# Keys and values in two sets of buffers and half a group ahead, in an eight-group decoder kernel on one core

## The chip, the cores and the metric

The kernel runs on one core of a Trainium2 chip. Its engines are TensorE (PE), VectorE (DVE), ScalarE (ACT), GpSimd (POOL) and SyncE (SP, which issues the DMAs); each takes its own instructions in order and waits on semaphores. The metric is the device time of one execution in microseconds. PE's granted clock is 2.4 GHz (1.00 in the rows) or 1.2 GHz (0.50).

## The reference

Two post-norm decoder layers over x of 16 x 128 x 256, with a context `ctx_2048` of the same shape. Each line is one of six stages:

```python
x = _layernorm(x + _L0_attn_ref(x, qkv, o_proj, gamma, beta))        # causal attention, one head of 256
x = _layernorm(x + _L0_xattn_ref(x, k, fside_S2_0, ctx, ctx, 8))     # long convolution, 8 x 8 products
x = _layernorm(x + _L0_ffn_ref(x, w1, g1, w2, g2, w3, g3))           # int8 activations, ternary weights
x = _layernorm(x + _L1_attn_ref(x, Wr, Wk, Wv, Wo, decay, ...))      # decayed running sum of k * v
x = _layernorm(x + _L1_xattn_ref(x, ctx, mask, Wq, bq, Wk, bk, ...)) # 16 query heads, 4 key/value heads of 128
x = _layernorm(x + _L1_ffn_ref(x, w_gating, w_linear))               # fp8 gated FFN
```

The cross attention of layer 1 is what the change touches most. Its keys and values come from the context alone; only the queries need x:

```python
q = (hidden_states @ Wq + bq)...; k = (encoder_hidden_states @ Wk + bk)...; v = (encoder_hidden_states @ Wv + bv)...
q = _rmsnorm(q, qn_w); k = _rmsnorm(k, kn_w)
probs = softmax(q @ k.T * scale + attention_mask); out = (probs @ v) @ Wo
```

The ternary weights of the layer-0 FFN are `round(tanh(w / mean|w|))`, that is -1, 0 or 1, times one scale.

## The kernel before

The 16 sequences go in 8 groups of 2 (GB = 2); a group has 256 rows. There are three stations, and each holds another group at the same time. Station a does a group's layer-0 attention and convolution (`front`), and later its last FFN (`ffn`, three groups behind: AHEAD = 4). Station c (`middle`) does the ternary FFN (steps c_) and the running sum (steps d_). Station e does the cross attention: `keys_queries` (letter q: keys, values, queries), `scores` for each sequence of the group (letters x and y) and `output` (letter o).

For every engine, each station is a generator that yields between steps, and `together` plays the generators in the order of a string of letters, `ORDER[engine]`. The strings are written out in the file (one letter a step) and set what stands behind what on each in-order engine. The eight PSUM banks are split: A0, A1 (banks 0, 1) for station a, C0, C1 (2, 3) for c, E0, E1 (4, 5) for the scores, EQ (6) for keys, values and queries, EY (7) for the output product.

Station q, one group before the change: two key products into EQ (L1159), DVE adds the bias into KX (L884), POOL squares KX into QS (L411), DVE sums (L887), POOL takes the power and scales KX (L414, L416); then the group's rows are turned (L966), the first quarter of the queries is made (L1166) with its sums of squares (L1171, L1177), the scaled keys are turned (L1224) and copied to KTX by ScalarE (L586), and the two value products follow (L1159, copied to VX in L595); then the other three quarters of queries. KX, KTX, VX and QS exist once. QS is also where ScalarE puts the squares of the queries. All steps of q go through the one bank EQ, each waiting for the last one to be read out.

Station c for a group: DVE scales and quantises the rows (L766 to L780), PE turns them (L1098), four pairs of matmuls make gate and value of a hidden quarter in C0 and C1 (L1111), each pair waiting for DVE to have read the last (c_h); ScalarE takes tanh (L536), DVE forms the hidden values (L788, L789); POOL multiplies by g3 (L394), DVE quantises (L794 to L806), PE turns and multiplies by w_dn (L1118, L1124), DVE adds and norms. Then the running sum: projections (L972, L1138), K1 from ScalarE, times the value projection on DVE (L828), times dinv on POOL (L402), running sum on PE (L1144), means (L1148, L1151), output projection and the second norm.

At the start the weights are loaded and prepared through two stage buffers that share memory with station e's tiles: the ternary weights as bf16 (L449, L454, L641) and the weights of the last FFN as fp8 (L469). `keep_clock` puts small matmuls on PE where it would be quiet; the last 56 of them stand right behind the last output product.

## Time and profile before

| | us |
|---|---|
| median of 3 runs | 922.15 |
| lowest and highest | 920.11, 922.54 |
| the profiled execution | 919.01 |
| its span, first to last instruction | 917.2 |
| PE busy | 832.2 (91%) |
| DVE, ACT, POOL busy | 685.5 (75%), 518.5 (57%), 297.4 (32%) |
| mean granted PE clock | 0.976 |

Start times in the rows count from the start of the span. A row of the order in time has start, duration, engine, line, operation, tiles written and read, and in square brackets the idle time before it with the releaser. Four fp32 matmuls show as eight records.

### The profile page before, as it was taken

How to read it: one execution, taken by the hardware profiler on the slowest of the kernel's cores; microseconds unless marked ns; L12 is line 12 of the kernel's file. 1: busy time of each engine (PE TensorE's matmuls, PEld its weight loads, DVE VectorE, ACT ScalarE, POOL GpSimd, SP SyncE). 2: the span in 40 equal slices, each digit the busy share in tenths (PEclk: the TensorE clock that was granted, in tenths of full speed). 3: DMA queues.
4: the chain of work that ended last, by engine and by line, in shares of the span. 5: the costliest groups of instructions: out<-in, count | busy, mean ns of one | idle time of the engine just before them, and what ended most of it. 6: DMA issues, size and time to landing. Idle time of an engine off the chain costs nothing.

```text
span 917.2 us, 14519 instructions
## 1 busy us (share of the span) xinstructions
PE 832.2 (91%) x5052; PEld 646.5 (70%) x5068; DVE 685.5 (75%) x1687; ACT 518.5 (57%) x1317; POOL 297.4 (32%) x314
## 2 busy tenths in 40 slices
PE   6866958999899999999999999999999998999984
PEld 5743845886687667876689677786689766686763
DVE  2777767978896887786968869687968979483544
ACT  4464127525436775358752695527863487576853
POOL 0426314522622252514233423351235423230110
PEclk9986979999999999999999999999999999999998
DMA  8780100010010000010001000000000000000000
GB/s 279 252 285 31 24 1 24 1 24 1 12 30 7 12 1 24 1 24 2 24 12 24 1 1 24 12 12 14 24 1 1 1 12 13 1 1 13 1 12 12
DMA packets 37063, 28.66 MB, mean 31 GB/s; under 512 B 18688, under 2 KB 34560, under 8 KB 36608
## 3 DMA queue, kind: packets, MB, share of 16 engines
q1 hardware_dynamic: 36992, 27.74, 9.8%
q8 instruction: 41, 0.67, 0.3%
q14 instruction: 30, 0.25, 0.1%
HBM read 25.64 MB, written 2.10 MB: 30 GB/s over the span
## 4 chain that ended last, share of the span: by engine, by line
PE 56%; DVE 27%; ACT 7%; issue 6%; POOL 2%; DMA 1%; DVEq 0%; SPq 0%; POOLq 0%; ACTq 0%
PE bank L1166 7%; PE bank L1262 6%; PE bank L972 5%; PE bank L1159 4%; PE bank L1251 4%; PE bank L1241 3%; DVE S L900 3%; PE bank L1073 2%; PE bank L1043 2%; PE bank L1041 2%; PE bank L1044 2%; PE bank L1246 2%; PE bank L1111 2%; PE bank L1171 2%; DVE S L907 2%
## 5 line engine op out<-in xcount | busy, mean ns | idle before, releaser
L606 ACT ACTIVATE S<-S,mx 128x128 f32<-128x128 f32 x256 | 99.5, 394 | 46.1 <-DVE mx L903 45.9
L1166 PE MATMUL bank<-XTE,w_xq 128*128 128x256 f32 x512 | 122.6, 382 | 1.4 <-ACT QA L565 0.7
L1262 PE MATMUL bank<-w_xo,OX 128*128 128x256 f32 x512 | 116.1, 380 | 0.9 <-ACT OX L615 0.9
L1166 PEld LDWEIGHTS bank<-XTE,w_xq 128*128 128x128 f32 x512 | 93.9, 190 | 17.5 <-ACT QA L565 3.1
L1262 PEld LDWEIGHTS bank<-w_xo,OX 128*128 128x128 f32 x512 | 95.0, 190 | 13.9 <-issue 2.1
L564 ACT ACTIVATE QS<-bank,per_partition_sb 128x256 f32<-128x256 f32 x128 | 60.6, 473 | 62.4 <-PE bank L1166 62.3
L338 POOL TENSOR_TENSOR rq<-vq,minus_half 128x8 f32<-128x8 f32 x32 | 53.7, 1679 | 123.3 <-DVE vq L879 123.2
L900 DVE SCALAR_TENSOR_TENSOR S<-bank,rq,xmask 128x128 f32<-128x128 f32 x256 | 71.7, 342 | 19.8 <-PE bank L1241 17.8
L236 POOL TENSOR_TENSOR prod<-XTA,ccolA 128x256 f32<-128x256 f32 x96 | 60.7, 664 | 45.0 <-PE bank L1044 25.0
L1241 PEld LDWEIGHTS bank<-KTX,QA 128*128 128x128 f32 x512 | 63.3, 192 | 12.3 <-issue 10.7
L1241 PE MATMUL bank<-KTX,QA 128*128 128x128 f32 x512 | 67.8, 278 | 1.0 <-ACT OX L615 0.9
L615 ACT ACTIVATE OX<-bank,bv_sb 128x512 f32<-128x512 f32 x64 | 44.0, 691 | 42.2 <-PE bank L1251 30.2
L1159 PE MATMUL bank<-w_xkv_sb,ccolE 128*128 128x512 f32 x128 | 62.2, 609 | 4.6 <-DMA w_xo<-in_L_xattn_Wo 3.4
L1251 PE MATMUL bank<-PT,VX 128*128 128x512 f32 x128 | 65.6, 603 | 0.3 <-ACT PT L610 0.3
L565 ACT ACTIVATE QA<-bank,per_partition_sb 128x256 f32<-128x256 f32 x128 | 60.8, 475 | 0.0
L394 POOL TENSOR_TENSOR H<-H,g 128x1024 f32<-128x1024 f32 x16 | 38.5, 2403 | 58.3 <-ACT Q L540 58.3
L338 POOL TENSOR_TENSOR rstd_c<-veps_c,minus_half 128x2 f32<-128x2 f32 x24 | 16.9, 705 | 111.0 <-DVE veps_c L667 98.2
L907 DVE TENSOR_TENSOR S<-S,rs 128x512 f32<-128x512 f32 x64 | 51.2, 801 | 2.2
L1043 PE MATMUL bank<-prod,taps_sb 128*128 128x128 f32 x256 | 51.2, 282 | 1.3 <-DVE Zc L720 1.3
L1044 PE MATMUL bank<-prod,taps_sb 128*128 128x128 f32 x256 | 50.4, 279 | 0.0
L606 ACT ACTIVATION_READ_ACCUMULATOR S<-S,mx 128x1 f32 x256 | 49.1, 192 | 0.0
L610 ACT ACTIVATE PT<-bank 128x512 f32<-128x512 f32 x64 | 37.8, 601 | 19.9 <-PE bank L1246 19.8
(225 smaller groups left out, 1852.5 us busy)
## 6 DMA issues: line engine op xcount, KB each, us to landing
xin<-in_x SPq DMA_DIRECT2D x8, 256.0 KB, 2.7
taps_sb<-in_taps SPq DMA_DIRECT2D x1, 2048.0 KB, 11.8
cnat<-in_ctx SPq DMA_DIRECT2D x8, 256.0 KB, 2.7
ccolA<-in_ctxT SPq DMA_DIRECT2D x32, 64.0 KB, 2.7
ccolE<-in_ctxT SPq DMA_DIRECT2D x16, 128.0 KB, 2.3
w_xq<-in_L_xattn_Wq SPq DMA_DIRECT2D x1, 2048.0 KB, 13.1
w_xo<-in_L_xattn_Wo SPq DMA_DIRECT2D x1, 2048.0 KB, 17.8
out_x<-X SPq DMA_DIRECT2D x8, 256.0 KB, 2.1
```

Of the source, the lines that this page charges most:

```text
L338: sig(gp.tensor_tensor(out, src, minus_half[:, 0:n], ALU.pow), name)
L565: ins = nc.scalar.activation(QA[:, n % 2, h], q, ACT.Identity, bias=bq[:, hh:hh + 1])
L606: ins = nc.scalar.activation(S[:, b, seq(h)], S[:, b, seq(h)], ACT.Exp, bias=mx[:, b, h:h + 1], accum_out=sm[:, b, h:h + 1])
L900: ins = nc.vector.scalar_tensor_tensor(s3[:, h], EB[b][:, seq(h)], rq[:, n % 2, b * XGROUP + h:b * XGROUP + h + 1], xmask[:], ALU.mult, AL ...
L907: sig(nc.vector.tensor_tensor(s3, s3, rs[:, b].unsqueeze(2).broadcast_to([P, XGROUP, P]), ALU.mult), f"e_p{b}")
L1043: nc.tensor.matmul(out[:, :, h], taps[:, hq * 4 + h, 0:P], mv_[:, 1], start=True, stop=False)
L1044: ins = nc.tensor.matmul(out[:, :, h], taps[:, hq * 4 + h, P:], mv_[:, 0], start=False, stop=True)
L1159: ins = nc.tensor.matmul(EQ[:], ccolE[:, k, b], w_xkv[:, k, v], start=k == 0, stop=k == HALVES - 1)
L1166: ins = nc.tensor.matmul(cols(EQ)[:, h], w_xq[:, k, hh * XDIM:(hh + 1) * XDIM], XTE[:, k], start=k == 0, stop=k == HALVES - 1)
L1241: ins = nc.tensor.matmul(EB[b][:, seq(h)], QA[:, n % 2, h, seq(b)], KTX[:, b, n], start=True, stop=True)
L1251: sig(nc.tensor.matmul(EB[b][:], VX[:, b, n * XDIM:(n + 1) * XDIM], PT[:, b], start=True, stop=True), f"e_o{b}")
L1262: ins = nc.tensor.matmul(rows(EY)[:, b], OX[:, h, b], w_xo[:, n * XGROUP + h], start=n == 0 and h == 0 and b == 0, stop=n == XKV - 1 and h ...
```

## The change

- KTX and VX exist twice, one set for even and one for odd groups (`KTX[g % 2]`, `VX[g % 2]`). The set for odd groups shares memory with the weight stages as before.
- `keys_queries` is split into `keys(g, half)` and `queries(g, n)`. `station_q` plays keys and values of groups 0 and 1 first, before any query; then, in each group g from 1 to 6, group g + 1's key products behind query quarter 1 and its key transposes and value products behind quarter 2. The waits are moved to match: the key sums e_vk of the next group are waited for by ScalarE before quarter 2.
- `w_gv` and `w_dn` are fp8 instead of bf16, with saturate=False where they are written.
- In group 0 the hidden quarters 1 and 3 go to E0 and EY instead of C0 and C1, so a quarter waits for the one two before it.
- K1 is multiplied by dinv on POOL first and by the value projection on DVE after it.
- All five order strings are new.

```diff
-        w_gv, w_dn = sb("w_gv", [2, HALVES, HIDDEN], BF), sb("w_dn", [FFN_K, DIM], BF)
+        w_gv, w_dn = sb("w_gv", [2, HALVES, HIDDEN], F8), sb("w_dn", [FFN_K, DIM], F8)
...
+        KTX, VX = (sb("KTX0", [GB, XKV, P]), t["KTX1"]), (sb("VX0", [GB, BANK]), t["VX1"])
...
+        def hidden_banks(g, j):
+
+            return (E0, EY) if g == 0 and j % 2 else (C0, C1)
+
+        def hidden_free(g, j):
+
+            return j - 2 if g == 0 else j - 1
...
+        def keys_made_with(g):
+
+            return g + 1 if 1 <= g < GROUPS - 1 else None
+
+        def station_q(keys, queries):
+            for g in range(2):
+                yield from keys(g, 0)
+                yield from keys(g, 1)
+            for g in range(GROUPS):
+                made = keys_made_with(g)
+                for n in range(XKV):
+                    yield from queries(g, n)
+                    if made and n in (1, 2):
+                        yield from keys(made, n - 1)
...
-                gp.wait_ge(sems["d_kv"], nth(g))
-                sig(gp.tensor_tensor(K1[:], K1[:], dinv[:].unsqueeze(1).broadcast_to([P, GB, DIM]), ALU.mult), "d_kvs")
+                gp.wait_ge(sems["d_k"], nth(g))
+                sig(gp.tensor_tensor(K1[:], K1[:], dinv[:].unsqueeze(1).broadcast_to([P, GB, DIM]), ALU.mult), "d_kd")
...
+                    if n == 0 and pr == 0 and g == 0:
+                        act.wait_ge(sems["e_vk"], nth(1))
+                    if n == 2 and pr == 0 and made:
+                        act.wait_ge(sems["e_vk"], nth(made))
...
-                    else:
-                        pe.wait_ge(sems["c_h"], nth(g, 2 * GB, j - 1))
+                    if hidden_free(g, j) >= 0:
+                        pe.wait_ge(sems["c_h"], nth(g, 2 * GB, hidden_free(g, j)))
...
+                    if g == 0:
+                        pe.wait_ge(sems["e_kTc"], nth(1, GB, 1))
+                    else:
+                        pe.wait_ge(sems["e_vq"], nth(g - 1, XKV, XKV - 1))
+                    transpose_rows(X[g % XBUF], EQ, "e_xT")
```

How the order strings move instructions, at three places. PE at the start, behind the last instruction of set-up (the turned decay, L960 before and L995 now). L1111 and L1146 are group 0's hidden quarters, L1159 and L1194 key and value products, L991, L972 and L999 (L1026, L1007, L1034) group 1's attention. Before:

```order
58 L960 MATMUL bank5<-ident,dscale 128x128 x2
59 L1159 MATMUL bank6<-w_xkv_sb,ccolE 128x512 x2
60 L1098 MATMUL bank2<-ident_bf,QQ 128x128 x8
61 L966 MATMUL bank0<-ident,Z 128x128 x4
62 L1159 MATMUL bank6<-w_xkv_sb,ccolE 128x512 x2
63 L1111 MATMUL bank2<-w_gv,QQ 128x512 x2
64 L1111 MATMUL bank3<-w_gv,QQ 128x512 x2
65 L991 MATMUL bank1<-XTA,w_qk 128x256 x4
66 L972 MATMUL bank0<-w_vo,XTA 128x256 x4
67 L999 MATMUL bank1<-XTA,QT 128x128 x4
68 L1111 MATMUL bank2<-w_gv,QQ 128x512 x2
69 L1111 MATMUL bank3<-w_gv,QQ 128x512 x2
```

and now:

```order
59 L1133 MATMUL bank2<-ident_bf,QQ 128x128 x8
60 L1194 MATMUL bank6<-w_xkv_sb,ccolE 128x512 x2
61 L1146 MATMUL bank2<-w_gv,QQ 128x512 x2
62 L1146 MATMUL bank3<-w_gv,QQ 128x512 x2
63 L1146 MATMUL bank4<-w_gv,QQ 128x512 x2
64 L1146 MATMUL bank7<-w_gv,QQ 128x512 x2
65 L1001 MATMUL bank0<-ident,Z 128x128 x4
66 L1194 MATMUL bank6<-w_xkv_sb,ccolE 128x512 x2
67 L1146 MATMUL bank2<-w_gv,QQ 128x512 x2
68 L1146 MATMUL bank3<-w_gv,QQ 128x512 x2
69 L1146 MATMUL bank4<-w_gv,QQ 128x512 x2
70 L1146 MATMUL bank7<-w_gv,QQ 128x512 x2
```

Two hidden quarters now stand next to each other, in four banks, ahead of group 1's attention. Further on, the value products and key transposes of group 0 and the key and value products of group 1 (L1194, L1224) stand between group 0's remaining steps.

POOL at the start, from group 1's convolution products (prod, L236 before and L260 now) to the second norm of group 0. Before:

```order
43 L236 TENSOR_TENSOR prod<-XTA,ccolA 128x256 x3
44 L378 TENSOR_TENSOR UA<-X1,SK 128x512
45 L338 TENSOR_TENSOR rstd_c<-veps_c,minus_half 128x2
46 L402 TENSOR_TENSOR K1<-K1,dinv 128x512
47 L338 TENSOR_TENSOR rstd_a<-veps_a,minus_half 128x2 x2
48 L338 TENSOR_TENSOR rstd_c<-veps_c,minus_half 128x2
49 L338 TENSOR_TENSOR rstd_c<-veps_c,minus_half 128x2
```

and now:

```order
40 L362 TENSOR_TENSOR rstd_c<-veps_c,minus_half 128x2
41 L437 TENSOR_TENSOR QS<-KX 128x1024
42 L260 TENSOR_TENSOR prod<-XTA,ccolA 128x256
43 L260 TENSOR_TENSOR prod<-XTA,ccolA 128x256 x3
44 L260 TENSOR_TENSOR prod<-XTA,ccolA 128x256
45 L260 TENSOR_TENSOR prod<-XTA,ccolA 128x256 x3
46 L426 TENSOR_TENSOR K1<-K1,dinv 128x512
47 L402 TENSOR_TENSOR UA<-X1,SK 128x512
48 L440 TENSOR_TENSOR rk<-vk,minus_half 128x8
49 L442 TENSOR_TENSOR KX<-KX,rk 128x1024
50 L362 TENSOR_TENSOR rstd_c<-veps_c,minus_half 128x2
51 L362 TENSOR_TENSOR rstd_c<-veps_c,minus_half 128x2
```

Group 1's key steps (L437, L440, L442) have come in, and group 0's first norm stands ahead of two thirds of group 1's convolution products instead of behind them.

PE at the end. L1262 and L1317 are output products (bank 7), L978 and L1013 the clock keepers, L1080 and L1115 the transposes and L1087 and L1122 the products of the last FFN. Before:

```order
1038 L1251 MATMUL bank5<-PT,VX 128x512
1039 L1262 MATMUL bank7<-w_xo,OX 128x256 x8
1040 L978 MATMUL bank6<-ident_bf 128x128 x56
1041 L966 MATMUL bank0<-ident,X2 128x128 x4
1042 L1073 MATMUL bank0<-w_gf,X8 128x512 x2
```

and now:

```order
1031 L1306 MATMUL bank5<-PT,VX1 128x512
1032 L1108 MATMUL bank0<-w_gf,X8 128x512 x2
1033 L1108 MATMUL bank1<-w_gf,X8 128x512 x2
1034 L1317 MATMUL bank7<-w_xo,OX 128x256 x8
1035 L1013 MATMUL bank6<-ident_bf 128x128 x56
1036 L1115 MATMUL bank0<-ident_bf,G16 128x128 x8
1037 L1115 MATMUL bank1<-ident_bf,G16 128x128 x8
1038 L1122 MATMUL bank0<-w_ln,A8T 128x256 x8
1039 L1122 MATMUL bank1<-w_ln,A8T 128x256 x8
1040 L1001 MATMUL bank0<-ident,X2 128x128 x4
```

The second half of group 6's last FFN now stands behind the last output product, ahead of group 7's FFN, whose first transpose (into bank 0, from X2) waits for group 6's norm.

## Rows read from the trace of the kernel before

**Rows 1.** Page, part 1: busy time and share of the span.

```profile
PE 832.2 (91%) x5052; PEld 646.5 (70%) x5068; DVE 685.5 (75%) x1687; ACT 518.5 (57%) x1317; POOL 297.4 (32%) x314
```

**Rows 2.** Stretches: length, busy time by engine (records), PE clock, DMA share, GB/s.

```profile
0.00:138.00 138.00, 97.99 (x621) 79.83 (x623) 90.53 (x217) 51.13 (x88) 45.01 (x62) 0.86 0.44 145
138.00:893.00 755.00, 721.89 (x4325) 558.43 (x4339) 584.65 (x1445) 459.02 (x1218) 251.01 (x250) 1.00 0.04 11
893.00:917.20 24.20, 12.37 (x110) 8.25 (x108) 10.35 (x25) 8.39 (x12) 1.39 (x2) 0.86 0.03 12
...
54.50:132.00 77.50, 55.70 (x274) 42.16 (x276) 54.97 (x132) 22.48 (x40) 29.88 (x34) 0.78 0.19 57
...
127.59:132.61 5.02, 5.02 (x26) 4.41 (x24) 3.60 (x10) 1.71 (x6) 0.70 (x2) 0.87 0.00 0
```

**Rows 3.** Order in time, group 0 through station c, to its queries.

```profile
54.49 1.29 DVE L766 TENSOR_TENSOR UG<-X,g 128x512 f32<-128x512 f32 x2
...
60.62 0.69 DVE L780 TENSOR_SCALAR QQ<-UG 128x1024 bf16<-128x1024 f32 x1
...
84.70 1.88 DVE L803 TENSOR_TENSOR fac<-fac,srms 128x1 f32<-128x1 f32 x1
...
87.47 0.69 DVE L806 TENSOR_SCALAR Q<-H 128x1024 bf16<-128x1024 f32 x1
...
105.38 0.73 DVE L672 TENSOR_SCALAR X<-UC,mv_c,rstd_c 128x256 f32<-128x256 f32 x2
...
130.73 0.74 DVE L672 TENSOR_SCALAR X<-UC,mv_c,rstd_c 128x256 f32<-128x256 f32 x2 [0.81 <-POOL rstd_c L338]
...
133.90 1.99 PE L1166 MATMUL bank<-XTE,w_xq 128*128 128x256 f32 x8 [0.69 <-ACT XTE L570]
```

**Rows 4.** PE's waits from 138 to 893 us: total, times, longest.

```profile
PE bank L1224 <- ACT KTX L586: 2.0, 3, 0.9
```

**Rows 5.** PE by group: count, busy us, mean ns, idle before; last, the chain.

```profile
L1159 PE MATMUL bank<-w_xkv_sb,ccolE 128*128 128x512 f32 x128 | 62.2, 609 | 4.6 <-DMA w_xo<-in_L_xattn_Wo 3.4 <-DVE vq L879 0.6 <-ACT KTX L586 0.3
...
L1073 PE MATMUL bank<-w_gf,X 128*128 128x512 fp8e4 x128 | 32.3, 379 | 2.1 <-ACT X L500 1.5 <-DVE F L742 0.5
L1111 PE MATMUL bank<-w_gv,QQ 128*128 128x512 bf16 x112 | 30.2, 387 | 7.5 <-DVE H L789 3.9 <-ACT QQ L531 2.9
...
L1224 PE MATMUL bank<-ident,KX 128*128 128x128 f32 x64 | 9.8, 275 | 2.0 <-ACT KTX L586 2.0
...
351.94 1.72 PE bank L1159 x4
```

**Rows 6.** POOL and DVE: steps of the keys, and the two that meet at 84 us.

```profile
L416 POOL TENSOR_TENSOR KX<-KX,rk 128x1024 f32<-128x1024 f32 x8 | 15.2, 1897 | 0.6
L411 POOL TENSOR_TENSOR QS<-KX 128x1024 f32<-128x1024 f32 x8 | 15.2, 1894 | 36.8 <-DVE KX L884 36.8
L414 POOL TENSOR_TENSOR rk<-vk,minus_half 128x8 f32<-128x8 f32 x8 | 13.7, 1711 | 10.1 <-DVE vk L888 10.1
...
L887 DVE TENSOR_REDUCE vk<-QS 128x8 f32<-128x1024 f32 x8 | 9.7, 1213 | 5.2 <-POOL QS L411 5.2
...
84.23 2.34 POOL L394 TENSOR_TENSOR H<-H,g 128x1024 f32<-128x1024 f32 x1
...
L803 DVE TENSOR_TENSOR fac<-fac,srms x16: 158/159/1953, 84.7 to 769.4; 128x1 f32<-128x1 f32 x16
```

**Rows 7.** Order in time at the end.

```profile
876.81 1.04 PE L1087 MATMUL bank<-w_ln,A8T 128*128 128x256 fp8e4 x8
...
893.20 3.29 PE L978 MATMUL bank<-ident_bf 128*128 128x128 bf16 x56
...
897.17 0.63 PE L966 MATMUL bank<-ident,X 128*128 128x128 f32 x4 [0.68 <-DVE X L672]
...
907.12 3.56 PE L1087 MATMUL bank<-w_ln,A8T 128*128 128x256 fp8e4 x16
...
913.79 0.73 DVE L672 TENSOR_SCALAR X<-UA,mv_g,rstd_g 128x256 f32<-128x256 f32 x2 [0.81 <-POOL rstd_g L338]
```

More of the change, by code:

```diff
@@ L406, in middle, with keys @@
                 yield from norm(g, "c", 1, 2)
-            def keys_queries(g):
+            def keys(g, half):
+                if half == 1:
+                    return
                 yield
@@ L616, in scores @@
                                              bias=bv[:, n:n + 1]), f"e_oc{b}")
-            together(ORDER["act"], s=set_up(), a=station_a(front, ffn), c=each_group(middle), q=each_group(keys_queries),
+            together(ORDER["act"], s=set_up(), a=station_a(front, ffn), c=each_group(middle), q=station_q(keys, queries),
                      x=each_group(lambda g: scores(g, 0)), y=each_group(lambda g: scores(g, 1)))
@@ L888, in keys_queries, with queries @@
                 sig(nc.vector.tensor_scalar(vk[:], vk[:], 1.0 / XDIM, 1e-6, ALU.mult, ALU.add), "e_vk")
-                yield from query_squares(0)
-                for n in range(1, XKV):
-                    yield from query_squares(n)
+            def queries(g, n):
+                yield
+                dve.wait_ge(sems["e_ssT"], nth(g, XKV, n))
+                if g or n >= 2:
+                    dve.wait_ge(sems["e_rq"], g * XKV + n - 1)
+                sums = EQ[:, 0:GB * P].rearrange("p (m r) -> p m r", r=QUARTER)[:, :, 0]
+                sig(nc.vector.tensor_scalar(vq[:, n % 2], sums, 1.0 / XDIM, 1e-6, ALU.mult, ALU.add), "e_vq")
             def scores(g, b):
@@ L918, in output @@
                 norm_out("e", UE, x)
-            together(ORDER["dve"], s=set_up(), a=station_a(front, ffn), c=each_group(middle), q=each_group(keys_queries),
+            together(ORDER["dve"], s=set_up(), a=station_a(front, ffn), c=each_group(middle), q=station_q(keys, queries),
                      x=each_group(lambda g: scores(g, 0)), y=each_group(lambda g: scores(g, 1)), o=each_group(output))
@@ L1154, in middle, with keys, product @@
                 project_rows(C1, lambda k, b: NT[:, b, k], lambda k: w_o1[:, k], "d_y")
-            def keys_queries(g):
-                def keys_values(v, b):
+            def keys(g, half):
+                def product(v, b):
                     for k in range(HALVES):
@@ new lines, in keys_turned @@
+                def keys_turned():
+                    for b in range(GB):
+                        yield
+                        if b == 1:
+                            pe.wait_ge(sems["e_kTc"], nth(g, GB, 0))
+                        elif g < 2:
+                            pe.wait_ge(sems["e_vc"], nth(g, GB, 1))
+                        else:
+                            pe.wait_ge(sems["e_vq"], nth(g - 1, XKV, 2))
+                        if b == 0:
+                            pe.wait_ge(sems["e_kn"], nth(g))
+                        for m in range(XKV):
+                            ins = nc.tensor.transpose(EQ[:, seq(m)], KX[:, b, m * XDIM:(m + 1) * XDIM], ident[:])
+                        sig(ins, "e_kT")
@@ new lines, in values @@
+                def values():
+                    for b in range(GB):
+                        yield
+                        if b == 1:
+                            pe.wait_ge(sems["e_vc"], nth(g, GB, 0))
+                        elif g < 2:
+                            pe.wait_ge(sems["e_kc"], nth(g, GB, 1))
+                        else:
+                            pe.wait_ge(sems["e_kTc"], nth(g, GB, 1))
+                        product(1, b)
+                if half == 0:
+                    yield from keys_made()
+                    if g < 2:
+                        yield from values()
+                else:
+                    yield from keys_turned()
+                    if g >= 2:
+                        yield from values()
@@ new lines, in queries @@
+                yield
+                pe.wait_ge(sems["e_qc"], nth(g, 2 * XKV, 2 * n + 1))
+                for h in range(XGROUP):
+                    ins = nc.tensor.matmul(EQ[h * QUARTER:(h + 1) * QUARTER, 0:GB * P], ones[:, 0:QUARTER], QS[:, h], start=True, stop=True)
+                sig(ins, "e_ssq")
+                yield
+                pe.wait_ge(sems["e_ssc"], nth(g, XKV, n))
+                for b in range(GB):
+                    ins = nc.tensor.transpose(EQ[:, seq(b)], SSQ[:, seq(b)], ident[:])
@@ L1240, in scores @@
                     for h in range(XGROUP):
[L1241 removed]
+                        ins = nc.tensor.matmul(EB[b][:, seq(h)], QA[:, n % 2, h, seq(b)], KTX[g % 2][:, b, n], start=True, stop=True)
                     sig(ins, f"e_sc{b}")
@@ L1268, in output @@
                         keep_clock(EQ, 56)
-            together(ORDER["pe"], s=set_up(), a=station_a(front, ffn), c=each_group(middle), q=each_group(keys_queries),
+            together(ORDER["pe"], s=set_up(), a=station_a(front, ffn), c=each_group(middle), q=station_q(keys, queries),
                      x=each_group(lambda g: scores(g, 0)), y=each_group(lambda g: scores(g, 1)), o=each_group(output))
```

267 lines of the change are left out of this document (120 added, 147 removed).

## The prediction, before the result was known

> **What bounds the kernel now.** I read the page first: TensorE (PE) is busy for 832.2 us, 91% of the span, VectorE (DVE) for 75% [rows 1]. The table of stretches says where the missing 9% lies. From 0 to 138 us PE is busy for 97.99, so idle for 40.0, at a mean granted clock of 0.86. From 138 to 893 us it is busy for 721.89 of 755, idle for 33.1 (4.4%), at full clock. In the last 24.2 us it is idle for 11.8 [rows 2]. The middle is a PE stage; start and end are chains. So an edit pays if it takes waiting out of the start or end, or if it puts PE work of the middle into waiting at the start; shortening a chain in the middle is worth at most its part of 33.1 us.
>
> The order in time shows the chain of the start, which runs through DVE. Station c takes group 0's rows at 54.49; its first quantised hidden half is there at 88.16 (start 87.47 plus 0.69); its first norm is written from 105.38 and its second from 130.73, right behind which group 1's station c starts; PE starts group 0's queries at 133.90 [rows 3]. From 54.5 to 132 us PE is busy for 55.70 of 77.5, at a clock of 0.78 [rows 2]. In the middle, from 138 to 893 us, the list of waits shows little before key and value steps: 2.0 us in all before the key transposes [rows 4].
>
> **The change, part by part.** My sum goes against the profiled execution, 919.0 us (span 917.2 and 1.8 around it). The median of the three runs is 922.15, 3.1 above; I put the difference onto the median.
>
> *Two groups' keys and values in front.* A group's eight products take 62.2 / 8 = 7.8 us of PE, its transposes 9.8 / 8 = 1.2 [rows 5]. Up to the start of group 0's queries PE now does, beyond what it did before, group 0's value products and key transposes and all of group 1's: (3.9 + 1.2) + (7.8 + 1.2) = 14.1 us by busy time. These sums count overlapping ends: a product of four records is 1.94 by this count and 1.72 on the chain [rows 5], so I take 14.1 x 1.72 / 1.94 = 12.5. Group 2's first projections and scores, 5.0 us on PE [rows 2], have moved behind. Net, 7.5 us of work leave the PE-bound part.
>
> *Group 0's hidden layer in four banks, and the order around it.* Before, each of four matmul groups waited for VectorE to finish the one before, with group 1's attention between. Now the first two run back to back, and quantising the first half comes ahead of group 1's residual. I walked the new order by hand with durations from the trace. Quantised input 60.4 (before 61.3 [rows 3]; a norm of group 1 no longer stands in it). First products end near 66, hidden quarters written at 67.0, 68.5, 73.5 and 74.9. Two things hold it up: ScalarE now has the weight copies behind the first activation, so the stage loads start about 5 us later, and POOL has group 0's key work (1.89 + 1.71 + 1.90 [rows 6]) between its two g3 products of 2.4. Still the quantised halves come at 79.5 and 86.3, the first before at 88.2, and the first norm at about 96 instead of 105.4. From there the new order is slower than the old: station d's steps share DVE with twelve convolution steps of group 1, which before were finished. On the other side K1 is multiplied by dinv (a POOL step) while PE makes the second projection, and not behind it, which saves about 1.2 on the chain. I get the second norm at 119 to 120 instead of 130.7, queries at 120.3 instead of 133.9, and group 1's station c at 121.5. Allowing for a half clock (1.2 instead of 2.4 GHz) on PE where it starts from quiet, for which the 0.78 of before stands, I take 11.5 us, bounds 6 and 14.
>
> *Less to fill with.* The work moved forward was filler behind 138 us. With 7.5 us of it gone and the chains earlier by unequal amounts (queries 13.6 us, group 1's station c 10, group 2's front hardly), some idleness returns. It can't be below 0 by this reason, nor much above the 7.5 and the spread of 4 to 5 between the chains, 12. I take 5, that spread.
>
> *Keys half a group ahead.* Number and kind of steps through bank EQ are the same, so PE's and DVE's sums stay. Scores of a group can start once its first queries are out. Gain at most 2 us or so, the waits of [rows 4]; the loss is a rival below. I take 0.
>
> *Ternary weights as fp8.* They are the moving operand. L1073 with fp8 and L1111 with bf16, both 512 columns, take 32.3 / 128 = 0.25 and 30.2 / 112 = 0.27 us busy [rows 5], so the two differ by 0.02 x 128 = 2.6 us over the kernel, part of which is the slower clock under the first ones. No row has mixed operands; a loss of that size is in the range.
>
> *The end.* Before, group 6's FFN was through when the last output product ended at 893.36; behind it came 56 clock keepers, then group 7's FFN at 897.17 [rows 7]. Now group 6's two transposes and two products stand between the keepers and group 7's FFN. The chain: last output product end + 3.2 (keepers) + 1.1 (transposes) + 0.7 and 1.02 (ScalarE, second half ends) + 1.04 (product) + 3.8 from the last product to the written norm (910.68 to 914.52 before [rows 7]) + 0.1 = 11.0 us, against 3.8 before: +7.1. The 3.1 us of PE work (1.06 and twice 1.04) leave the part ahead. Net +4.0 if PE bounds there, +7.1 if it doesn't. I take 4.
>
> **The sum:** -11.5 - 7.5 + 5 + 0 + 0 + 4.0 = -10.0 us. That is 909.0 for a profiled execution and 912.1, say **912 us**, for the median.
>
> **A rule weighed.** In the trace one DVE step of one element per partition (fac, L803; median 159 ns, longest 1953) lasts 1.88 us at 84.70: it ends at 86.58, just when POOL's product over H (84.23 plus 2.34) ends [rows 3, 6]. The change puts 5.5 us more of POOL work into the start, so up to two such holds (3.8 us) can be added on the chain. By this the sum would be -6.2, 916. The Trainium skill says in GPSIMD Engine Reference, section Specifications, that POOL's SBUF interface is shared with VectorE, with contention for instructions that have two SBUF inputs. The trace agrees for this row. I keep it as a rival, because the row has a median of 159.
>
> **The rivals.**
> - *The fill holds.* Group 0's queries and scores come together with group 1's hidden layer and group 2's front, so no idleness returns (-5), and the waits before key steps go (-2): 922.15 - 17.0 = 905. For it: three independent stations are open from 121 us on. Against: all three lean on DVE, 75% busy [rows 1].
> - *The fill is lost.* Idleness of 12 instead of 5 comes back: 922.15 - 3.0 = 919, at the edge of what is measurable.
> - *Keys in the middle of a group stall the queries (slower).* ScalarE may not write the squares of query quarter 2 before the next group's key sums are out, and the transposes wait for scaled keys: 1.89 + 1.38 + 1.71 + 1.90 = 6.9 us of POOL and DVE work [rows 6], the 1.38 being DVE's reduction of 1.21 and a small step, in groups 1 to 6, with the remaining scores of the group queued behind on PE. Before, this wait lay at the group's start, where the last group's scores covered it. At 3 us uncovered in each of six groups: +18, 930. It decides from 10.0 / 6 = 1.7 us a group. Against: PE has waited for little in the middle.
> - *The keys don't get out of the way.* Group 0's rows can't be turned into queries before group 1's keys are through bank EQ; POOL scales them behind two convolution products and dinv. By my walk they are through at 116, 3 us ahead. If they end 4 us late, 916.
> - *POOL holds VectorE*, above: 916.
>
> **How the numbers follow.** Forecast 0.41, fill holds 0.22, fill lost 0.15, slower by stalled queries 0.12, keys in the way 0.06, POOL holds 0.04. A measurement tells 0.3%, 2.8 us, from no change. Faster: 0.41 + 0.22 + 0.06 + 0.04 = 0.73; same 0.15; slower 0.12. The range goes from 903 (fill holds, 2 us of the startup's upper bound) to 925 (fill lost, the fp8 loss and the end at +7.1); it leaves out the slower case and little else.
>
> **What would show it.** In the changed profile: group 0's queries start near 120 us and the stretch before it has PE idle of about 20 and not 40 us; PE's idle time in the middle near 38; group 7's FFN starts 11 us behind the end of the last output product. If queries start at 130 or later, the walk is wrong. If they start at 120 and the time doesn't fall, the fill is. If PE waits for QS or KX in every group, the slower rival holds.

## The result: 900.4 us, and the profile of the changed kernel

The changed kernel takes 900.38 us (median), the kernel before 921.89 in the same comparison: a ratio of 0.977, interval 0.9745 to 0.9786. It is faster, as forecast, but by 21.5 us and not by 10, and so below the low end of the range (903). One of its four executions took 4810.06 us and counts in the median but not in the ratio; the other three, 899.28 to 900.97, have a median of 899.80, so differences below that are taken from 900.38 would be 0.6 us more from there. The profiled execution has a span of 897.5 us against 917.2, 19.7 less.

First the page of the changed kernel, part 1 (busy time, share of the span, instructions), which answers [rows 1]:

```profile
PE 825.7 (92%) x5068; PEld 642.1 (72%) x5068; DVE 692.7 (77%) x1687; ACT 515.9 (57%) x1315; POOL 296.2 (33%) x314
```

TensorE still bounds the kernel. Where the time went is read from stretches cut at the same events in both kernels: 54.5 us (station c takes group 0's rows), the start of group 0's queries, the end of the last output product, the end. Up to 54.5 us both are alike. The columns are those of [rows 2]. First before:

```profile
54.50:133.90 79.40, 56.91 (x284) 43.14 (x285) 56.83 (x134) 23.96 (x43) 30.92 (x36) 0.79 0.18 56
133.90:893.36 759.46, 725.05 (x4344) 560.89 (x4360) 588.43 (x1459) 460.75 (x1222) 251.01 (x250) 1.00 0.04 11
893.36:917.20 23.84, 12.01 (x109) 8.00 (x105) 10.35 (x25) 8.39 (x12) 1.39 (x2) 0.86 0.03 12
```

Then the changed kernel:

```profile
54.50:128.06 73.56, 54.11 (x297) 38.27 (x297) 59.84 (x137) 26.28 (x47) 33.80 (x38) 0.94 0.23 67
128.06:866.76 738.70, 717.12 (x4315) 559.00 (x4316) 589.12 (x1447) 454.52 (x1215) 245.69 (x248) 0.99 0.04 10
866.76:897.50 30.74, 16.32 (x141) 10.21 (x137) 14.50 (x38) 9.63 (x14) 2.47 (x3) 0.84 0.05 18
```

The start is 5.8 us shorter, the middle 20.8 us, the end 6.9 us longer. In the middle, TensorE is busy 7.9 us less (725.05 to 717.12) and idle 12.8 us less: 759.46 - 725.05 = 34.4 before, 738.70 - 717.12 = 21.6 now. The prediction had idle time rising by 5 there. That is the miss to explain. (The trace before lacks 16 records of L1111, 5052 against 5068 weight loads [rows 1]; by the gaps at their places they would fill between 1 and 2 us of the 34.4, so it is not made by them.) TensorE's busy time there fell by less than forecast, 7.9 us and not 10.6 (7.5 moved to the front, 3.1 to the end).

The order in time of the start on VectorE, which answers [rows 3]:

```profile
60.41 0.69 DVE L815 TENSOR_SCALAR QQ<-UG 128x1024 bf16<-128x1024 f32 x1
...
72.68 1.22 DVE L917 TENSOR_REDUCE vk<-QS 128x8 f32<-128x1024 f32 x1 [2.01 <-POOL QS L437]
73.93 1.05 DVE L918 TENSOR_SCALAR vk<-vk 128x8 f32<-128x8 f32 x1
...
79.69 2.10 DVE L836 TENSOR_TENSOR deq<-amax,srms 128x1 f32<-128x1 f32 x1
...
83.26 0.69 DVE L842 TENSOR_SCALAR Q<-H 128x1024 bf16<-128x1024 f32 x1
...
89.11 0.69 DVE L842 TENSOR_SCALAR Q<-H 128x1024 bf16<-128x1024 f32 x1
...
98.73 2.23 DVE L707 TENSOR_SCALAR X<-UC,mv_c,rstd_c 128x256 f32<-128x256 f32 x2
...
124.79 0.73 DVE L707 TENSOR_SCALAR X<-UC,mv_c,rstd_c 128x256 f32<-128x256 f32 x2
```

The chain has the links that the prediction walked, each later than walked: the quantised input is through at 61.1 (walked: 60.4), the quantised halves at 84.0 and 89.8 (79.5 and 86.3); the first norm starts at 98.7 (96), the second at 124.8 (119 to 120), the queries at 128.06 (120.3). From the start of the quantised input to the queries it takes 67.65 us, against 73.28 before (60.62 to 133.90 [rows 3]).

TensorE's order in time goes on:

```profile
128.06 3.78 PE L1275 MATMUL bank<-XTE,w_xq 128*128 128x256 f32 x8 [1.82 <-ACT XTE L618]
...
133.50 3.72 PE L1275 MATMUL bank<-XTE,w_xq 128*128 128x256 f32 x8 [0.81 <-ACT QA L630]
```

Eight such records took 1.99 us before [rows 3]. The granted clock is 0.50 from 128.06 to 136.00, where before it is 1.00 from 133.90 on: the new order has little on TensorE right ahead of the queries (0.66 us of work from 124 to 128.06), the old one had group 1's attention there. These 7.94 us hold 7.1 us of busy time, of which the half clock costs about 3.6 (an estimate: the same products took about half in the kernel before). That is more than the 2.7 us by which the fall in busy time fell short.

### The profile page after: what moved, and what is told of

It is laid out like the page before. It is cut to its first block, busy times and chain, and to the rows that moved or that the text cites. A ratio compares the mean times of both kernels' runs of the same rounds, so it can differ in the third digit from the quotient of the medians.

```text
span 897.5 us, 14530 instructions
## 1 busy us (share of the span) xinstructions
PE 825.7 (92%) x5068; PEld 642.1 (72%) x5068; DVE 692.7 (77%) x1687; ACT 515.9 (57%) x1315; POOL 296.2 (33%) x314
## 4 chain that ended last, share of the span: by engine, by line
PE 61%; DVE 21%; ACT 9%; issue 5%; DMA 1%; POOL 1%; SPq 0%; POOLq 0%; DVEq 0%; ACTq 0%
PE bank L1317 9%; PE bank L1275 8%; PE bank L1007 5%; PE bank L1194 4%; PE bank L1306 4%; PE bank L1296 4%; PE bank L1078 2%; PE bank L1301 2%; PE bank L1079 2%; PE bank L1076 2%; PE bank L1108 2%; DVE amax L830 2%; DVE S L935 1%; PE bank L1280 1%; ACT S L641 1%
## 5 line engine op out<-in xcount | busy, mean ns | idle before, releaser
L1275 PE MATMUL bank<-XTE,w_xq 128*128 128x256 f32 x512 | 126.2, 390 | 5.4 <-ACT QA L630 2.7
L1317 PE MATMUL bank<-w_xo,OX 128*128 128x256 f32 x512 | 116.0, 380 | 0.0
L1275 PEld LDWEIGHTS bank<-XTE,w_xq 128*128 128x128 f32 x512 | 96.2, 194 | 22.8 <-ACT QA L630 5.6
L1317 PEld LDWEIGHTS bank<-w_xo,OX 128*128 128x128 f32 x512 | 95.4, 190 | 14.0 <-issue 1.8
L260 POOL TENSOR_TENSOR prod<-XTA,ccolA 128x256 f32<-128x256 f32 x96 | 60.4, 661 | 26.6 <-DVE prod L260 16.8
L1194 PE MATMUL bank<-w_xkv_sb,ccolE 128*128 128x512 f32 x128 | 62.7, 613 | 1.1 <-ACT KTX L591 0.9
L1078 PE MATMUL bank<-prod,taps_sb 128*128 128x128 f32 x256 | 50.0, 277 | 1.5 <-DVE SK L747 1.0
L1079 PE MATMUL bank<-prod,taps_sb 128*128 128x128 f32 x256 | 49.5, 275 | 0.0
L755 DVE TENSOR_TENSOR Zc<-bank,ccolA 128x512 f32<-128x512 f32 x64 | 43.7, 683 | 7.3 <-PE bank L1079 4.4
```

The source lines that it names most:

```text
L1078: nc.tensor.matmul(out[:, :, h], taps[:, hq * 4 + h, 0:P], mv_[:, 1], start=True, stop=False)
L1079: ins = nc.tensor.matmul(out[:, :, h], taps[:, hq * 4 + h, P:], mv_[:, 0], start=False, stop=True)
L1194: ins = nc.tensor.matmul(EQ[:], ccolE[:, k, b], w_xkv[:, k, v], start=k == 0, stop=k == HALVES - 1)
L1275: ins = nc.tensor.matmul(cols(EQ)[:, h], w_xq[:, k, hh * XDIM:(hh + 1) * XDIM], XTE[:, k], start=k == 0, stop=k == HALVES - 1)
L1317: ins = nc.tensor.matmul(rows(EY)[:, b], OX[:, h, b], w_xo[:, n * XGROUP + h], start=n == 0 and h == 0 and b == 0, stop=n == XKV - 1 and h ...
```

## The experiments

Order strings are quoted only where a few letters say what moved. The start of the same instructions varies by several microseconds between executions (last section), so a loss there is read from the quantised input on. "Middle" is always from the start of group 0's queries to the end of the last output product.

**The two borrowed banks.** Group 0's hidden layer goes back to two banks, all order strings as they are.

```diff
-            return (E0, EY) if g == 0 and j % 2 else (C0, C1)
+            return (C0, C1)
-            return j - 2 if g == 0 else j - 1
+            return j - 1
```

> The changed kernel with group 0's hidden layer back in two banks (C0, C1) instead of four, same order. Each of its four matmul groups waits for VectorE to have read the one before. If the borrowed banks carry the earlier start (5.8 us measured), the start of group 0's queries comes 4 to 6 us later and the whole 2 to 5 us later, 902 to 905. If VectorE sets the pace there anyhow (a hidden quarter takes it 1.4 us and TensorE under a microsecond), under 1.5 us is lost: 900 to 902.

Measured: 909.98 us, ratio to the kernel before 0.988 (0.9855 to 0.9904), so 9.6 us over the changed kernel. The order in time of its VectorE shows where:

```profile
62.12 0.69 DVE L815 TENSOR_SCALAR QQ<-UG 128x1024 bf16<-128x1024 f32 x1
...
80.53 0.68 DVE L824 SCALAR_TENSOR_TENSOR SW<-SW,bank 128x512 f32<-128x512 f32 x1
...
95.45 0.69 DVE L842 TENSOR_SCALAR Q<-H 128x1024 bf16<-128x1024 f32 x1
```

From quantised input to first quantised half it takes 33.3 us, against 22.9 with four banks. Queries start at 140.15, and the middle is 738.85 us long against 738.70: the whole loss, 12.1 us between the two profiles, lies in the start and is carried to the end undiminished. The quantised input itself comes 1.7 us later, which the edit doesn't touch; the link to the first half accounts for the other 10.5. Both readings in the expectation were too low. I had counted what VectorE needs for a quarter, 1.4 us. TensorE's order in time in the same kernel shows a round trip instead:

```profile
70.73 1.78 PE L1146 MATMUL bank<-w_gv,QQ 128*128 128x512 fp8e4 x4 [2.38 <-DVE H L825]
...
75.43 1.03 PE L1146 MATMUL bank<-w_gv,QQ 128*128 128x512 fp8e4 x4
82.14 1.86 PE L1146 MATMUL bank<-w_gv,QQ 128*128 128x512 fp8e4 x4 [5.69 <-DVE H L825]
```

The second and the fourth quarter wait for VectorE (2.38 and 5.69 us), and behind the wait their products run at half clock (1.78 and 1.86 us for four, at a granted clock of 0.53 and 0.50, against 1.03 us at 1.00). The second wait is long since VectorE had the sums of the key squares ahead of the third quarter. The order strings stand as they were made for four banks, with two quarters next to each other, so this is what the banks are worth in this order; an order made for two banks wasn't tried.

**Group 1's keys not in front.** Only group 0's keys and values are made in front; group 1's are made among group 0's queries. Where a step didn't have to move, it kept its place.

```diff
-            return g + 1 if 1 <= g < GROUPS - 1 else None
+            return g + 1 if g < GROUPS - 1 else None
...
-            for g in range(2):
-                yield from keys(g, 0)
-                yield from keys(g, 1)
+            yield from keys(0, 0)
+            yield from keys(0, 1)
```

> The changed kernel with only group 0's keys and values in front; group 1's stand among group 0's queries, as those of the later groups do. The order of all other steps is that of the changed kernel. The prediction's term for the work moved to the front: group 1's share is 9.0 of 14.1 us, so about 8 us of TensorE work go back behind the start. If that work filled idle time in front (the prediction's view), the time is 5 to 8 us longer, 905 to 908, with queries of group 0 starting earlier or at the same 128. If the idle time in the middle takes the work in again (there are 21.6 us of it), under 3 us: 900 to 903.

Measured: 913.57 us, ratio 0.992 (0.9902 to 0.994), 13.2 us over the changed kernel. Its middle and end:

```profile
127.60:881.35 753.75, 726.01 (x4336) 562.78 (x4337) 592.22 (x1451) 456.34 (x1219) 251.96 (x251) 0.99 0.04 10
881.35:912.20 30.85, 16.47 (x141) 10.50 (x139) 14.67 (x38) 9.79 (x14) 2.47 (x3) 0.84 0.05 18
```

Queries start at 127.6, and 66.7 us behind the quantised input where the changed kernel takes 67.65: group 1's keys in front cost the start about 1 us. The middle is 15.1 us longer: 8.9 us are work (726.01 against 717.12), and 6.2 us are *more* idle time (27.7 against 21.6). The list of TensorE's waits in its middle names them (total, times, longest):

```profile
PE bank L1193 <- DVE KX L913: 3.6, 1, 3.6
...
PE bank L1272 <- DVE KX L913: 0.9, 1, 0.9
PE bank L1193 <- ACT KTX L593: 0.8, 1, 0.8
PE bank L1193 <- ACT VX L601: 0.7, 1, 0.7
PE bank L1272 <- ACT VX L601: 0.7, 1, 0.7
```

These five, 6.7 us together, are waits of or behind key and value steps (L1193 is the product for keys and values, L1272 the query projection behind it). The list of the changed kernel's middle, which goes down to 0.4 us, has none of them. So group 1's keys and values, made here, bring waits beside their work, and in front they cost next to none. The prediction's bound, that idle time can't fall when this work goes, fails on this.

How much of it lies in the steps and how much in their place is not shown. The same steps of groups 2 to 7 stand in the changed kernel's middle without a listed wait, and in the kernel before, key and value steps account for 3.2 us of TensorE's waits in the whole middle (2.0 before the key transposes [rows 4], 1.2 before L1159). Group 1's stand at 161 to 206 us, among group 0's queries, in strings that are otherwise made for a kernel without them there. Another place for them was not tried, so a less fitting order remains a rival for the 6.2 us.

One more reading. Middle and end together are 753.75 + 30.85 = 784.6 us here, and 759.46 + 23.84 = 783.3 in the kernel before. With group 1's keys out of the front, the rest of the change (two sets of buffers, later groups' keys half a group ahead, new orders) gains nothing behind the start in this order: the middle is 5.7 us shorter than before (753.75 against 759.46), and the end 7.0 us longer.

**Where the later groups' keys stand.** Three pairs of kernels. In each, both have an order made by the same procedure from durations of the trace; one has the program of the changed kernel, the other makes keys and values of group g (from 2 on) between the last queries of group g-1 and the first of its own. Both sets of buffers stay.

```diff
                 for n in range(XKV):
                     yield from queries(g, n)
-                    if made and n in (1, 2):
-                        yield from keys(made, n - 1)
+                if made:
+                    yield from keys(made, 0)
+                    yield from keys(made, 1)
```

> The changed kernel (keys half a group ahead, two sets of buffers, four banks for group 0) with all five order strings made anew by a search of my own; computation and steps are the same, only their interleaving differs. It is the partner of n_start, whose order was made by the same search. If the change's own order strings were the source of the 12.8 us of TensorE idle time that left the middle, another order has no reason to keep it: 905 to 920. If the structure gives the slack, an order from an unrelated search keeps it: 885 to 900, with idle time in the middle at or below the 21.6 us of the changed kernel.

> As n_after, with an order from the same search, but the keys and values of group g (g from 2) are made between the last queries of group g-1 and the first of group g, not among the queries of g-1. Buffers stay double. Theory A (keys in the middle of a group fill waits, and free the start of each group from a chain of 6.9 us of POOL and DVE steps): 8 to 12 us longer than n_after, with waits of TensorE before key transposes or at the first queries of a group. Theory B (where the keys stand doesn't matter, only that the order is good): within 3 us of n_after.

> As n_after, with the order of a second, independent search (another seed). It measures how much of the time hangs on the search's luck: if order luck is a few us, 908 to 920.

> As n_start (keys and values of a group between the last queries of the group ahead and the first of its own), with the order of a second, independent search. Theory A (keys among the queries give 10 us or more by structure): slower than both n_after and n_after2, 920 to 935. Theory B (the 14.5 us between n_after and n_start were the luck of one order): it lies among them, 908 to 920.

> The changed kernel with an order that keeps its own as the priority, but lets a step go ahead where, on durations from the trace, the one in front of it isn't ready. Partner of g_start. If the changed kernel's order is near the best for its structure, this is 0 to 10 us slower, 900 to 910.

> Same rule and same priorities as g_after, with the keys and values of a group (from 2 on) between the last queries of the group ahead and its own first ones. Theory A (keys half a group ahead give slack by structure): 7 to 15 us slower than g_after, as in the two pairs before. Theory B: within 4 us of it.

Measured, in us; the ratio is to the kernel before.

| pair | keys among the queries | keys at the group's start | difference of medians | of middle and end, by the traces |
|---|---|---|---|---|
| n | 914.46 (0.993; 0.9909 to 0.9948) | 928.91 (1.010; 1.0063 to 1.0131) | 14.4 | 19.7 |
| n, second order | 919.72 (1.000; 0.9985 to 1.0007) | 927.20 (1.007; 1.0059 to 1.0089) | 7.5 | 2.0 |
| g | 928.81 (1.009; 1.0062 to 1.0126) | 965.16 (1.049; 1.0447 to 1.0526) | 36.3 | 37.1 |

The last column leaves the start out: in the second pair 7.1 of the difference is a later start (queries at 140.7 and not 133.6). The middle of the third pair:

```profile
131.80:895.40 763.60, 723.55 (x4312) 559.58 (x4313) 587.20 (x1445) 453.17 (x1215) 244.42 (x247) 0.99 0.04 10
```

```profile
131.60:938.60 807.00, 743.05 (x4344) 566.31 (x4345) 592.59 (x1464) 459.15 (x1222) 245.93 (x250) 0.97 0.04 10
```

The first fence is the one with keys among the queries, the second the one with keys at the start of the group: 64 us of idle time in the middle against 40. In the list of waits of the second, TensorE waits 9.1 us before key and value steps for ScalarE's copy of the turned keys (6.0 at L1193, 3.1 at L1223); that of the first has no such row.

Two things follow. All three differences have one sign, so keys half a group ahead are no burden and may be a help; but 2.0, 19.7 and 37.1 are no size, and this stays open. And one program with four orders (the changed kernel's and three of mine) has 769.4, 780.3, 783.0 and 794.4 us in middle and end: the order strings alone are worth 11 to 25 us. My expectation that an unrelated order would keep the small idle time (at or below 21.6 us, and 885 to 900 in all) held for none: the first n kernel comes nearest in the middle with 24.3 us, g has 40.1. The 914.46 of the first lies in the range that was given for order strings as the source, 905 to 920.

**The dinv product.** POOL's product of K1 and dinv stands behind VectorE's product of keys and values again.

```diff
-                gp.wait_ge(sems["d_k"], nth(g))
+                gp.wait_ge(sems["d_kv"], nth(g))
...
-                dve.wait_ge(sems["d_kd"], nth(g))
+                dve.wait_ge(sems["d_k"], nth(g))
...
-                pe.wait_ge(sems["d_kv"], nth(g))
+                pe.wait_ge(sems["d_kd"], nth(g))
```

> The changed kernel with POOL's product of K1 and dinv (1.26 us) behind VectorE's product of keys and values again, as in the kernel before; order strings as in the changed kernel. The prediction gave the swap 1.2 us on group 0's chain and nothing elsewhere: +1 to +1.5 us, 901 to 902. If in each group this chain is where waits of TensorE come from, 1.2 us in each of eight groups would show: up to +6, 906.

Measured: 904.74 us, ratio 0.984 (0.9806 to 0.9868), 4.4 us over the changed kernel, between the two expectations. TensorE's wait ahead of the state product, as that line's own view gives it, in this kernel and in the changed one (the first row is the line's operations, the second what its engine waited for, us and times):

```profile
L1179 PE MATMUL bank<-upto,K x64: 275/275/377, 111.7 to 773.6; 128*128 128x128 f32 x64
...
  POOL K L426: 6.3, 4
```

```profile
L1179 PE MATMUL bank<-upto,K x64: 273/275/377, 109.6 to 767.6; 128*128 128x128 f32 x64
...
  DVE K L864: 1.5, 2
```

The swap takes 4.8 us of waits at this line away over eight groups. The middle is 3.4 us shorter with it (738.70 against 742.10), and from quantised input to queries it takes 67.65 us against 68.65, 1.0 less. The prediction gave it 1.2 us in the start, which is borne out, and looked no further.

**The start's key steps.** This one was meant to let group 0's hidden quarters and g3 products go ahead of its key squares.

The first letters of POOL's string; those of TensorE, VectorE and ScalarE have changes of this size too.

```diff
-sasaaaaaaacsaqcqcaaacqaacaqccacaqaac
+sasaaaaaaacasqcqcaaacaqcaaqccacaqaac
```

> As e_tail (keepers behind group 6's FFN, its second FFN half ahead of the residual sum), and in the start four short pieces of the order strings changed, one on each of TensorE, VectorE, ScalarE and POOL: group 0's key squares and sums (POOL 1.89 and 1.66 + 1.90 us, VectorE 1.21 + 1.05) give way to group 0's hidden quarters and its g3 products. In the changed kernel they stood between them: POOL started the g3 product at 72.6 although the quarters were there at 70.1, VectorE waited 2.0 us for POOL's squares with a hidden quarter queued behind, and deq lasted 2.10 us. If this is the part of the start that the prediction missed (5.8 us gained instead of 11.5), group 0's queries start 4 to 7 us earlier than e_tail's 127.2, and the time is 890 to 893 against 896.3. If the start is bound by something else (the 20 us of station d behind the first norm), the queries stay at 126 to 128 and the time at 895 to 897.

Measured: 899.25 us, ratio 0.977 (0.9754 to 0.9783), which is 3 us *more* than e_tail (below, from which it is made), queries at 130.1 instead of 127.2. But the edit didn't do what the expectation says: in the strings that ran, letters moved around the squares and not past them, and the trace has them where they were (VectorE waits 2.01 us for POOL's squares at 75.81, deq lasts 2.10 us again). From quantised input to first half it takes 25.4 us, against 23.2 in e_tail. So the run says nothing on the holds in the start; it says that other swaps of neighbours there made this link longer. (Of the queries' 2.9 us, 1.8 are a later quantised input.) What the squares cost by standing first is open.

**The end.** Two steps that the trace of the changed kernel shows late: the keepers stand ahead of group 6's last four TensorE steps and not ahead of group 7's FFN, and VectorE computes group 6's second half (L782) only at 868.78, behind group 7's residual sum, though it could at 867.01.

```diff
@@ FFN, behind the product of b
+                    if g == GROUPS - 2 and b == GB - 1:
+                        pe.wait_ge(sems["e_vq"], nth(GROUPS - 1, XKV, XKV - 1))
+                        keep_clock(EQ, 56)
@@ output
-                    if g == GROUPS - 1 and n == XKV - 1:
-                        pe.wait_ge(sems["e_vq"], nth(g, XKV, XKV - 1))
-                        keep_clock(EQ, 56)
@@ the last letters for VectorE
-yxayxaaaaoaoaaaaaaaaaaaa
+yxayxaaaaaooaaaaaaaaaaaa
```

> The changed kernel with its end undone in two small ways: the 56 clock keepers behind the last output product stand behind the last product of group 6's FFN instead, and VectorE computes group 6's second FFN half (f_a) ahead of the residual sum of group 7. If the end costs what the prediction says (+7.1 us of chain behind the last output product, of which the wait for that half and the keepers are 3 to 4), and the half clock under group 7's first FFN products (6.13 us instead of 3.61) comes from the quiet ahead of them, the time falls by 4 to 6 us to 894 to 896. If the clock doesn't follow the keepers: 1.5 to 3 us less than the changed kernel, 897 to 899. If the end is hidden: 900.

> As e_tail, with 92 clock keepers instead of 56. In e_tail TensorE stood still for 2.0 us between the keepers and the transposes of group 7's FFN, and the FFN's first products took 5.30 us, against 3.61 in the kernel before. If quiet ahead of them costs the clock, 36 more keepers of 58 ns fill it and the products go back to 3.6: 1 to 2 us less than e_tail, 894.5 to 895.5. If the keepers now hold up the transposes: 0 to 1 us more.

Measured: e_tail 896.27 us (892.37 to 898.24), ratio 0.973 (0.9697 to 0.9758); e_tail2 898.36, ratio 0.976 (0.9723 to 0.9799). TensorE's order in time at the end of the changed kernel, of e_tail and of e_tail2:

```profile
863.07 3.69 PE L1317 MATMUL bank<-w_xo,OX 128*128 128x256 f32 x16
866.60 3.29 PE L1013 MATMUL bank<-ident_bf 128*128 128x128 bf16 x56
...
877.53 0.92 PE L1001 MATMUL bank<-ident,X 128*128 128x128 f32 x4 [3.96 <-issue]
879.42 6.13 PE L1108 MATMUL bank<-w_gf,X 128*128 128x512 fp8e4 x16 [0.97 <-ACT X L527]
```

```profile
862.44 3.69 PE L1320 MATMUL bank<-w_xo,OX 128*128 128x256 f32 x16
...
870.02 3.29 PE L1013 MATMUL bank<-ident_bf 128*128 128x128 bf16 x56
875.32 0.63 PE L1001 MATMUL bank<-ident,X 128*128 128x128 f32 x4 [2.01 <-issue]
877.01 5.30 PE L1108 MATMUL bank<-w_gf,X 128*128 128x512 fp8e4 x16 [1.06 <-ACT X L527]
...
885.61 2.14 PE L1122 MATMUL bank<-w_ln,A8T 128*128 128x256 fp8e4 x16 [0.18 <-ACT A8T L547]
```

```profile
866.09 3.69 PE L1320 MATMUL bank<-w_xo,OX 128*128 128x256 f32 x16
...
873.66 5.30 PE L1013 MATMUL bank<-ident_bf 128*128 128x128 bf16 x92
878.97 0.63 PE L1001 MATMUL bank<-ident,X 128*128 128x128 f32 x4
880.58 3.61 PE L1108 MATMUL bank<-w_gf,X 128*128 128x512 fp8e4 x16 [0.98 <-ACT X L527]
...
888.02 3.19 PE L1122 MATMUL bank<-w_ln,A8T 128*128 128x256 fp8e4 x16
```

From the end of the last output product to the end of the span it takes 30.7 us in the changed kernel, 28.2 in e_tail and 28.0 in e_tail2. So e_tail gains 2.6 us in the end, less than the 4 to 6 expected: the transposes come 1.6 us sooner (9.2 us behind the output product and not 10.8), and the first products take 5.30 us instead of 6.13 (granted clock 0.68 and 0.58), still far from 3.61. With more keepers, and TensorE busy up to the transposes, these take 3.61 (at 1.00), as the expectation says, but the last products (L1122) fall to half clock instead, 3.19 us at 0.59 and not 2.1: little is left of it. e_tail2's median is higher because its profiled start is later (queries at 133.0 and not 127.2) with not one instruction changed there; its end is the shorter of the two. e_tail has the lowest median that was measured, 4.1 us below the changed kernel (3.5 below its 899.80); of that the traces assign 2.6 us to the end.

## The prediction, step by step

*What bounds it.* Right: TensorE in the middle, VectorE's chain in the start. The share of idle time in the middle fell from 4.5% to 2.9%.

*Start, -11.5.* The direction and the mechanism were right, the size was 5.8 (its own lower bound was 6), and 5.6 from the quantised input on. Three links of the walk were short. First quantised half: 22.9 us behind the quantised input and not 19.1; in it VectorE stands 2.01 us for POOL's key squares with a hidden quarter queued behind, and deq takes 2.10. From first to second norm: 26.06 us and not 23.5; in it the first norm itself takes 2.23 instead of 0.73. From the second norm to the queries: 3.27 us and not 0.3 to 1.3, where rows 3 have 3.17 in the kernel before (130.73 to 133.90); the walk left most of this link out. The rule weighed in the prediction, POOL holding VectorE, was put at up to 3.8 us and kept out of the sum "because the row has a median of 159". Held operations in this chain are L918 (1.05, median 0.19), L836 (2.10, median 0.16) and the pair of L707 (2.23, mostly 0.73), 4.3 us over their medians. The kernel before had 1.7 of the kind in its chain (L803, 1.88 [rows 3]), so 2.6 came in, within the rival's "up to 3.8". For the first two the hold ends with POOL's instruction (last section). For L836, whose two inputs are both in SBUF, the trace agrees with what the Trainium skill says of contention (GPSIMD Engine Reference, section Specifications). L918 has one tensor input; the same row names instructions in a 2-port perf mode too, and no run here shows whether it ran in one. So the rival's mechanism is there; the time of 916 that it gave isn't, because of the next two terms. The banks were not priced by themselves. Without them, in this order, the link from input to first half is 10.5 us longer and queries start at 140.15, later than before the change.

*Two groups' keys in front, -7.5.* The size of the work is right: for group 1, 9.0 us forecast, 8.9 measured (g1_inside against the changed kernel). Nearly free in front, as assumed. What the prediction left out is that the middle now opens at half clock (about 3.6 us, an estimate); its busy time fell by 7.9 us and not by 10.6.

*Less to fill with, +5, bounds 0 and 12.* This is the step that failed, and the bound "can't be below 0 by this reason" with it: idle time in the middle fell by 12.8 us. The reason took the moved steps for filler that is missed when it goes. In g1_inside, putting group 1's back adds 6.2 us of idle time to 8.9 us of work: 15.1 us of the middle, where the two terms together gave 2.5 for all that was moved. TensorE's waits in the middle say where idle time went. Before:

```profile
PE bank L1246 <- DVE S L907: 6.8, 9, 1.6
PE bank L1118 <- DVE Q L806: 5.9, 6, 1.7
PE bank L1098 <- DVE QQ L780: 3.6, 3, 1.8
PE bank L1111 <- ACT QQ L531: 2.9, 2, 2.0
```

The changed kernel, the same steps as far as its list has them:

```profile
PE bank L1153 <- DVE Q L842: 3.5, 7, 0.9
PE bank L1301 <- DVE S L942: 2.9, 5, 0.9
```

Turning the softmax's rows (L1246, now L1301) waits 3.9 us less, turning the quantised hidden rows (L1118, now L1153) 2.4 less, and turning the quantised input and the first hidden products behind it (L1098, L1111) 6.5 less (the list has them no more). Key and value steps give only 3.2. Against that, waits for VectorE between hidden quarters rose by 2.6 (2.2 to 4.8), and those before the query products by 3.8 (1.4 to 5.2). So most of the fall is in steps that the change doesn't touch except by what now stands around them. No run isolates it; that orders of one program differ by 11 to 25 us makes the order strings the first candidate. That is argued, not shown. The rival "the fill holds" (905) was nearest to the result: it had key steps' waits go and no idleness come back, but it too had nothing beyond that 2 us.

*Keys half a group ahead, 0.* Not refuted: middle and end with group 1's keys back are those of before within 1.3 us, and moving the later keys back costs 2 to 37 us, depending on the order. The slower rival (queries stalled, +18) didn't come; in the list of waits of the changed kernel's middle, which goes down to 0.4 us, no row is a key step's.

*Ternary weights as fp8, 0.* Right as far as rows show; no run isolates it. L1146 in the changed kernel:

```profile
L1146 PE MATMUL bank<-w_gv,QQ 128*128 128x512 fp8e4 x128 | 32.6, 379 | 4.8 <-DVE H L825 4.8
```

0.255 us each for L1146, where bf16 took 30.2 / 112 = 0.27 with some records missing [rows 5]. What fp8 does is make room: by the declarations the second set of buffers takes 8192 bytes a partition, and the narrower weights free 6144.

*dinv, 1.2 within the start.* Right for the start (1.0), mis-sized by leaving the other groups out: 4.4 us in all.

*End, +4.0 (a chain of +7.1, less 3.1 of work taken from the part ahead).* The chain is right: the end is 6.9 us longer. One link was not foreseen: group 7's first FFN products take 6.13 us, at half clock behind 4 us of quiet, 2.5 more than before. The sum comes out all the same since the kernel before had its half clock further on: its last products take 3.56 us at 0.52 [rows 7], those of the changed kernel 2.08 at 1.00. That part is luck.

By stretch, forecast against measured: start -11.5 and -5.8; middle -7.5 + 5 - 3.1 = -5.6 and -20.8; end +7.1 and +6.9. The start missed by 5.7 one way, the middle by 15.2 the other (17.8 of idle time, less 2.7 of work): -10.0 and -19.7 by the profile.

## What to carry to other kernels

Steps that are moved out of a full stage into a waiting one can take waits with them, here up to 6.2 us beside 8.9 of work, so don't bound their worth by their busy time: ask of each whether it is filler (ready long before it runs) or a chain (it waits on other engines), and which waits stand around it in the order in which it runs. Look also at what clock the next stage starts with once work ahead of it has moved. Price every part of a change in all the places where it runs, not only in the one for which it seems made. Where an order is written out by hand, its interleaving can weigh as much as the structure it serves, so compare structures under more than one order.

## What the runs showed of the hardware that was not expected

- A VectorE operation with its operands in SBUF can be held until POOL's current instruction ends. In the changed kernel deq (L836, one element a partition, median 160 ns) ran from 79.69 to 81.79 while POOL's product over H ran to 81.77; L918 (median 194 ns) ran 1051 ns, from 73.93 to 74.98, under a POOL product that ended at 74.95. Reductions over 128x1024 under POOL's products took their usual 1.22 and 1.21 us (72.68 and 78.44). POOL's two products:

```profile
72.60 2.35 POOL L418 TENSOR_TENSOR H<-H,g 128x1024 f32<-128x1024 f32 x1
...
79.42 2.35 POOL L418 TENSOR_TENSOR H<-H,g 128x1024 f32<-128x1024 f32 x1
```

- The start of one and the same program varies by several microseconds. The changed kernel, e_tail and e_tail2 are alike up to the end of the middle, yet the quantised input is there at 60.41, 59.26 and 62.67 us, and queries start at 128.06, 127.2 and 133.0. A change of the start of under 6 us should be read from a link of the chain (input to first half: 22.9, 23.2 and 23.0 in the three), not from the span.
- Keepers move the half clock as much as they remove it. 36 more of them brought 5.30 us of products down to 3.61 and the last ones up from 2.14 to 3.19.
